# Second attention: in eight of 32 slots the maximum also writes negated scores to SBUF, and the exponential reads them there

## The reference

```python
q = (x @ Wq + bq).reshape(b, h, dh, t)
k = (x @ Wk + bk).reshape(b, h, dh, t)
v = (x @ Wv + bv).reshape(b, h, dh, t)
attn = jnp.einsum('bhdt,bhds->bhts', k, v) * temperature
attn = jax.nn.softmax(attn, axis=-1)
out = jnp.einsum('bhdt,bhts->bhds', q, attn)
...
x = x + _L0_attn_a_ref(_layernorm(x), ...)
x = x + _L0_ffn_ref(_layernorm(x), W_fc, W_proj)
x = x + _L0_attn_b_ref(_layernorm(x), ...)
x = x + _L0_ffn_ref(_layernorm(x), W_fc, W_proj)
```

## Time and profile before

| what | value |
|---|---|
| runs | 2755.39, 2760.02, 2760.64 us; median 2760.02 us |
| profiled execution | span 2751.0 us from its first to its last instruction; no other time is shown for it |
| attention B, one tile in the steady part | 40.38 us |
| stage 1450 to 2751 us, busy | PE 1233.88, DVE 1194.69, ACT 1200.71, POOL 551.03 us of 1301 |

### The profile page before, as it was taken

The page is one execution under the profiler, slowest core; times in us unless marked ns, Lnnn a source line. Parts: engine busy times, 40 slices in busy tenths (PEclk is TensorE's granted clock), DMA queues, the critical chain, the costliest instruction groups (busy, mean ns, idle before and its releaser), DMA issues. The chain is left out here.

```text
span 2751.0 us, 38753 instructions
## 1 busy us (share of the span) xinstructions
PE 2361.1 (86%) x12438; PEld 1033.2 (38%) x12672; DVE 2511.8 (91%) x2596; ACT 2549.7 (93%) x4763; POOL 1282.7 (47%) x1897
## 2 busy tenths in 40 slices
PE   5788888877787778778778999999999999999997
PEld 2244444443343344344332333333333333333334
DVE  5899999999999999999988999999999999999994
ACT  4899999999999999999988999999999999999994
POOL 0146666655455455555542344434434444443445
PEclk8899999999999999999999999999999999999999
DMA  7521212233311111111111111111111111111110
GB/s 212 121 64 52 69 52 70 60 89 81 73 29 35 43 35 36 36 43 29 43 37 50 38 42 43 38 36 45 42 31 47 43 32 42 43 38 37 44 28 16
DMA packets 190929, 140.77 MB, mean 51 GB/s; under 512 B 92163, under 2 KB 177669, under 8 KB 190726
## 3 DMA queue, kind: packets, MB, share of 16 engines
q1 hardware_dynamic: 190534, 137.76, 18.8%
q10 hardware_dynamic: 192, 0.52, 0.1%
HBM read 92.04 MB, written 41.94 MB: 49 GB/s over the span
## 5 line engine op out<-in xcount | busy, mean ns | idle before, releaser
L1040 DVE TENSOR_REDUCE nmax<-score 128x1 f32<-128x1024 f32 x1024 | 1196.4, 1213 | 101.4 <-PE score L812 95.5
L1013 DVE TENSOR_REDUCE nmax<-score 128x1 f32<-128x1024 f32 x1024 | 1211.0, 1219 | 75.7 <-PE score L750 66.1
L1239 ACT ACTIVATE big<-score,nmax 128x1024 f32<-128x1024 f32 x1024 | 1138.3, 1120 | 69.2 <-DVE nmax L1013 58.2
L1282 ACT ACTIVATE score<-score,nmax 128x1024 f32<-128x1024 f32 x1024 | 1119.4, 1099 | 45.0 <-DVE nmax L1040 43.8
L812 PE MATMUL score<-big,shared 128*128 128x512 bf16 x1956 | 615.3, 395 | 273.9 <-ACT score L1282 236.6
L750 PE MATMUL score<-shared 128*128 128x512 bf16 x1906 | 574.3, 384 | 65.1 <-ACT big L1239 32.7
L731 PE MATMUL bank_g<-big,qw 128*32 128x512 f32 x4096 | 545.7, 606 | 1.0 <-ACT qcol L1267 1.0
L750 PEld LDWEIGHTS score<-shared 128*128 128x128 bf16 x2048 | 138.1, 97 | 594.3 <-ACT big L1239 536.4
L812 PEld LDWEIGHTS score<-big,shared 128*128 128x128 bf16 x2048 | 130.0, 98 | 566.0 <-ACT score L1282 474.0
L706 PEld LDWEIGHTS bank_f<-norms,w_fc_sb 128*128 128x128 f32 x2048 | 278.8, 192 | 75.7 <-ACT hid L1204 37.0
L706 PE MATMUL bank_f<-norms,w_fc_sb 128*128 128x128 f32 x2048 | 297.4, 279 | 10.7 <-ACT hid L1204 9.7
(11 more groups left out here) (145 smaller groups left out, 1653.8 us busy)
## 6 DMA issues: line engine op xcount, KB each, us to landing
shared<-q_parts SPq DMA_DIRECT2D x256, 64.0 KB, 2.5
shared<-kb_parts SPq DMA_DIRECT2D x256, 64.0 KB, 2.3
shared<-vb_parts SPq DMA_DIRECT2D x256, 64.0 KB, 2.3
big<-k_parts SPq DMA_DIRECT2D x48, 192.0 KB, 5.2
big<-k_parts SPq DMA_DIRECT2D x24, 256.0 KB, 7.8
kb_parts<-pieces SPq DMA_DIRECT2D x96, 64.0 KB, 1.6
vb_parts<-pieces SPq DMA_DIRECT2D x96, 64.0 KB, 1.6
shared<-in_x SPq DMA_DIRECT2D x32, 128.0 KB, 2.5
```

The lines of the kernel that those rows point to most:

```text
L1013: v.tensor_reduce(nmax[:, par, c // NCH, c % NCH:c % NCH + 1], score_b(turn, c)[:, :], AX.X, ALU.max, negate=True).then_inc(max_b, 1)
L1040: v.tensor_reduce(nmax[:, par, c // NCH, c % NCH:c % NCH + 1], score_a(turn, c)[:, :], AX.X, ALU.max, negate=True).then_inc(max_a, 1)
L1239: a.activation(expo[:, c // NCH, (c % NCH) * CH:(c % NCH + 1) * CH], score_b(turn, c)[:, :], ACT.Exp, bias=nmax[:, par, c // NCH, c % NCH: ...
L1282: a.activation(s[:, :], s[:, :], ACT.Exp, bias=nmax[:, par, c // NCH, c % NCH:c % NCH + 1], accum_out=esum[:, par, c // NCH, c % NCH:c % N ...
```

## The change

In slots 3, 6, 9, 12, 19, 22, 25 and 28 (`STAGED`) DVE's `tensor_reduce` is replaced by a `tensor_scalar` that reads the same scores, multiplies by -1, takes the minimum with the largest float, writes the 128 x 1024 result into that slot's part of `expo`, and gives the minimum over the row as its accumulator output into `nmax`. The exponential of such a slot reads that part of `expo` and writes it in place, with scale -1. PE's scores of slots 6, 9, 12, 15, 22, 25, 28 and 31 now wait for `max_b` in place of `exp_b`. Since DVE now writes `expo`, it waits for `prod_done` in slots 3 and 19.

```diff
+STAGED = [3, 6, 9, 12, 19, 22, 25, 28]
+INF = float(np.finfo(np.float32).max)
...
+        def row_chunk(c):
+
+            return expo[:, c // NCH, (c % NCH) * CH:(c % NCH + 1) * CH]
...
-                need(pe, exp_b, CPT * i + c - NBUF + 1)
+                need(pe, max_b if (c - NBUF) % CPT in STAGED else exp_b, CPT * i + c - NBUF + 1)
...
-                v.tensor_reduce(nmax[:, par, c // NCH, c % NCH:c % NCH + 1], score_b(turn, c)[:, :],
-                                AX.X, ALU.max, negate=True).then_inc(max_b, 1)
+                if c in STAGED:
+                    if c == STAGED[0]:
+                        need(dve, prod_done, H * (i - 1) + HALF)
+                    if c == STAGED[len(STAGED) // 2]:
+                        need(dve, prod_done, H * i)
+                    v.tensor_scalar(row_chunk(c), score_b(turn, c)[:, :], -1.0, INF, ALU.mult, ALU.min,
+                                    accum_out=nmax[:, par, c // NCH, c % NCH:c % NCH + 1]).then_inc(max_b, 1)
+                else:
+                    v.tensor_reduce(nmax[:, par, c // NCH, c % NCH:c % NCH + 1], score_b(turn, c)[:, :],
+                                    AX.X, ALU.max, negate=True).then_inc(max_b, 1)
...
-                a.activation(expo[:, c // NCH, (c % NCH) * CH:(c % NCH + 1) * CH], score_b(turn, c)[:, :],
-                             ACT.Exp, bias=nmax[:, par, c // NCH, c % NCH:c % NCH + 1],
+                staged = c in STAGED
+                a.activation(row_chunk(c), row_chunk(c) if staged else score_b(turn, c)[:, :],
+                             ACT.Exp, bias=nmax[:, par, c // NCH, c % NCH:c % NCH + 1], scale=-1.0 if staged else 1.0,
```

## The result

The changed kernel takes 2735.36 us (median of 4 runs, 2731.68 to 2738.36) against 2757.7 us for the one before (4 runs, 2753.35 to 2760.64): the ratio is 0.991, with a 95% interval of 0.989 to 0.993. That is 22.3 us less; 15.7 were forecast, 2744.3 us as a time, in a range of 2731 to 2766.

The account below looks back on a forecast made before the run. No engine alone bounds it; PE, DVE and ACT are coupled by waits round a 40.38 us tile. Slots 28 and 12 give 0.26 + 0.28 = 0.54 us, times 29 tiles 15.7: 2760.0 - 15.7 = 2744.3 us, range 2731 to 2766.

Parts of the forecast that it names:

- The rival that all of PE's excess would go: Idle time over 0.36 us before weight loads of slots 28, 12 and 22 all goes: 1.00 a tile, 2731; chance 0.10.
- the tie at the statistics: After slot 24, DVE's statistics start 0.03 us after POOL's sum, which ends the copied product's transfers; both paths arrive together.
- Nothing from slots 18 to 24: Nothing won between slots 17 and 24 comes out, since copy and transfers don't move; slot 22's earlier release gains nothing.
- Slot 28 gives 0.35 - r: PE's scores from slot 28 gain 0.35 us, limited by slot 26's exponential, less slot 25's dearer maximum; 0.26 with r 0.09.
- slot 12 gives 0.28: PE starts slot 12's scores 0.28 us earlier, moving slot 14's maximum from 2035.65 to 2035.37 if DVE can follow.
- r: Extra time on DVE for the accumulator's read-out of a staged maximum: taken as 0.09 us, bounds nothing to 0.20.
- Even where nothing holds it: After a slot without a product, PE's weight load has 0.36 us idle regardless (slot 15); only what exceeds that counts.
- the signs that the prediction named: Tile some 39.85 us, slots 12 and 28 idle 0.36, slot 29 following slot 26's exponential, statistics 0.03 after POOL's sum, read-outs costing 0.09.
- the second rival: The read-out on DVE eats the gain, r 0.19 to 0.30, or an unseen wait takes over: 2754.5 to 2765.5; chance 0.20.
- The slower rival: DVE's staged maximum is held at its SBUF write beside busy POOL, 0.43 us each: 2792; chance 0.15.

Follow-up runs that it names:

- the cost alone: Changed kernel with the dearer maximum and exponential kept, but PE's scores of every slot waiting for the exponential again: 2760.61 us against 2760.27 before, ratio 1.0007.
- the run with late statistics: Changed kernel with the residual's row statistics moved two slots later on DVE, behind slots 26 and 27: 2719.28 us against 2760.27 before, ratio 0.9868.

## Why the prediction was right, and where it wasn't

**That PE's wait pays only on the path round the tile: right.** The six slots without 9 and 25 gave 0.00 us a tile, and the cost alone left the time where it was. The rival that all of PE's excess would go, 1.00 us a tile, fell. Its condition was that the tie at the statistics gives way; the run with late statistics brought that about, and there the tile fell by 1.00 us (40.40 to 39.40), though slot by slot it came from other places than the rival had it (slots 22 and 23 gave 0.09 us, not 0.26).

**Nothing from slots 18 to 24: right**, and shown twice: by the stretch that stayed at 7.7 us, and by the run that took the wait away and won 0.32 us more. That the tie was one of transfers also explains why each late sum went into the time whole, which I hadn't priced.

**Slot 28 gives 0.35 - r, slot 12 gives 0.28:** measured 0.32 in the stretch with slot 28, where 0.26 was forecast, and 0.36 in that with slot 12, where 0.28 was. The sum of 0.54 was low by 0.12 in this tile and by 0.14 in the median one. One term was mis-sized: **r, taken as 0.09, is nothing or nearly so**. The read-out of 83 ns starts with its successor (2126.46 both, 2129.94 both), and the next maximum starts 1.14 us after a staged one (2128.80 to 2129.94), as after a plain one: 1.14 is the median for both where DVE doesn't stand idle, 159 and 443 times. With 30 staged slots it is 1.15 after a staged one and 1.13 after a plain one, so r is at most 0.02. It lay at its lower bound, for which the prediction had 0.63 a tile; but r entered only the term of slot 28, and there it explains 0.06: 0.35 was due by the prediction's formula with r at nothing, and 0.32 came. The Trainium skill's two instructions ("VectorE: DVE Perf Modes", section "Two Vector instructions with no wait between them") are there in the trace, 256 of each; what they cost is a matter of overlap, and here they cost next to nothing.

**"Even where nothing holds it" was wrong.** The 0.36 us of idle time before slot 15's weight load, from which I counted the excess, was itself a wait for the exponential of slot 12, which started at 2034.22 in that tile, 1.26 us ahead of the load at 2035.48. Before the change that exponential and the loads of slots 8 and 10 are

```profile
2027.64 0.11 PEld L750 LDWEIGHTS score<-shared 128*128 128x128 bf16 x2 [0.84 <-ACT big L1239]
...
2029.65 0.11 PEld L750 LDWEIGHTS score<-shared 128*128 128x128 bf16 x2 [0.84 <-ACT big L1239]
...
2034.22 1.11 ACT L1239 ACTIVATE big<-score,nmax 128x1024 f32<-128x1024 f32 x1
```

and after it the loads of such a slot run on from those ahead:

```profile
2143.35 0.55 PEld L759 LDWEIGHTS score<-shared 128*128 128x128 bf16 x4 [0.84 <-ACT big L1257]
...
2145.32 0.11 PEld L759 LDWEIGHTS score<-shared 128*128 128x128 bf16 x2 [0.84 <-ACT big L1257]
```

From slot 8 to slot 10 it is 1.97 us, before it was 2.01 (2027.64 to 2029.65). In the median tile slots 8 to 10 give 0.05 us by this, and slots 11 to 13 give 0.32 in place of 0.28. These two make the 0.08 that the stretch with slot 12 gave over the forecast, which r can't explain. Of the signs that the prediction named, then, the idle time before the loads of slots 12 and 28 fell to 0.12 us and not to 0.36, and nothing starts 0.09 later; but slot 29's load starts 1.26 us after slot 26's exponential, and the statistics still start 0.03 us after POOL's sum, both as forecast (medians).

**The same step hid a larger error.** I set five of the eight releases at nothing "on the path", slots 15 and 31 among them. Alone that is so; but a gain at slot 12 or 28 puts the next wait on that buffer, 15 or 31, on the path. Had the change staged only the two slots that my sum paid for, I would have forecast 2744, and 2746 came in that run, by luck: the tile fell by 0.24, not by 0.54, and the first tiles made up for it. The forecast for the change came near because it releases the followers too.

**The size: 22.3 us measured, 15.7 forecast.** By the one tile above, steady tiles make 29 x 0.66 = 19.1 of it. The second and third tile gave 4.7 in the profiled pair, and late tiles took 4.9 back (6.8 - 1.9). That makes 18.9; the stage's slots took 1293.4 us in the profiled execution after and 1312.7 before, 19.3 less. The 3 us left to 22.3 are within the spread of the runs, 7 us for either kernel. So part of the nearness is luck: what the first tiles gave and what the late ones took nearly cancel. Why the second and third tile gained was not tried. Some bounds of the second rival are also off the prediction's own formula, by about 1 us: 0.98 - 4r gives 2753.6 at r = 0.19 and 2766.4 at 0.30, not 2754.5 and 2765.5. Nothing hangs on it.

**The slower rival: did not happen.** The maximum that writes its row beside a busy POOL lasts 1216 ns on the mean of 256; the 0.43 us by which two scalings with both ends in SBUF differ have no counterpart. This agrees with the exception that the Trainium skill makes for the form with an accumulator output ("SBUF — State Buffer", section "Who interferes with whom"), though these runs can't tell it from the source being PSUM.

## What to carry to other kernels

When three engines hand buffers round in a ring, a wait is worth its length only if it lies on the path that closes the period; follow that path once round, and then look at the next user of the same buffer, since it inherits the gain. A tie within hundredths of a microsecond between an engine and a side chain of transfers is a wall for any gain ahead of it: move the consumer of the side chain later first. And take an idle time for a floor only after looking whether its end, too, stands a fixed distance after another engine's work.

## What the runs showed of the hardware

- On DVE, a scaling of 128 x 1024 float32 from PSUM to SBUF with an accumulator output takes 1216 ns, as a reduction to one column does (1219 ns). Its read-out is a row of its own of 83 ns that delays the next instruction by next to nothing: a maximum that follows starts 1.14 us after the scaling, as after a reduction (medians of the changed kernel).
- On ACT, an exponential of the same size with a bias column takes 1158 ns from SBUF and 1118 ns from PSUM, and where PE waits for it most of the 40 ns are paid: its weight loads start 1.29 us after the exponential in place of 1.26, and a tile takes 0.10 us more in the run with the cost alone.
- PE's weight loads for a slot that follows a slot without a product join the loads ahead when nothing holds them, 0.12 us idle in place of 0.36, and the pair of slots takes 1.97 us in place of 2.01.
